# Rotary attention: probabilities turned by VectorE in 32x32 blocks, values multiplied in 32-row tiles, one head per group

## The reference, cut to what matters

```python
xn = layernorm(layernorm(x)) * ln_gamma + ln_beta
q, k, v = split(xn @ w_qkv)                      # 16 heads of 64 each
q, k = rope(q[1:]), rope(k[1:])                  # position 0 stays as it is
dots = einsum('bhqd,bhkd->bhqk', q, k) * 64 ** -0.5
attn = softmax(dots, axis=-1)
out = einsum('bhqk,bhkd->bhqd', attn, v)
x = x + out.reshape(B, N, 16 * 64) @ w_out       # then the other three layers
```

## Time and profile before

| What | Value |
|---|---|
| median of 3 runs | 1472.25 us (1471.01 to 1474.55) |
| the profiled execution's own time | 1474.61 us |
| its span | 1471.4 us |
| mean granted TensorE clock over the span | 0.923 |
| first to last row maximum of the rotary layer | 35.9 to 894.2 us |
| last addition of the rotary layer | 903.64 to 904.06 us |

### The profile page before, as it was taken

The page is one execution under the profiler, slowest core; times in us unless marked ns, Lnnn a source line. Parts: engine busy times, 40 slices in busy tenths (PEclk is TensorE's granted clock), DMA queues, the critical chain, the costliest instruction groups (busy, mean ns, idle before and its releaser), DMA issues. The chain is left out here.

```text
span 1471.4 us, 25634 instructions
## 1 busy us (share of the span) xinstructions
PE 1295.3 (88%) x8965; PEld 918.6 (62%) x8966; DVE 785.1 (53%) x1375; ACT 884.4 (60%) x1567; POOL 269.0 (18%) x200
## 2 busy tenths in 40 slices
PE   4999999999999999999999996279179999999885
PEld 2777777777777776777777774246156455554443
DVE  6555554545554653554554554235357667666616
ACT  4777776777777776777776774323022556555643
POOL 2313312322312321320330330300400000000000
PEclk8999999999999999999999998589675999999987
DMA  6435334334434523523533532611134411011001
GB/s 182 103 92 124 80 81 114 92 75 111 112 75 99 120 61 93 122 61 92 122 80 73 122 86 63 213 41 48 46 93 141 148 48 51 19 42 30 16 1 34
DMA packets 60223, 125.43 MB, mean 85 GB/s; under 512 B 10961, under 2 KB 31826, under 8 KB 59986
## 3 DMA queue, kind: packets, MB, share of 16 engines
q1 hardware_dynamic: 58690, 120.12, 31.7%
q0 software_dynamic: 1424, 3.67, 0.9%
HBM read 31.15 MB, written 13.70 MB: 30 GB/s over the span
## 5 line engine op out<-in xcount | busy, mean ns | idle before, releaser
L529 DVE TENSOR_REDUCE a_negmax<-a_score 128x1 f32<-128x1024 f32 x257 | 314.0, 1222 | 397.0 <-PE a_score L355 397.0
L464 ACT ACTIVATE a_probs_T<-a_tr 128x512 f32<-128x512 f32 x514 | 279.9, 601 | 214.7 <-PE a_tr L361 211.2
L470 ACT ACTIVATE a_probs<-a_score,a_negmax 128x1024 f32<-128x1024 f32 x256 | 288.3, 1126 | 6.8 <-DVE a_negmax L529 6.7
L361 PE MATMUL a_tr<-ident,a_probs 128*128 128x128 f32 x2056 | 269.6, 274 | 0.4 <-ACT a_probs_T L464 0.4
L361 PEld LDWEIGHTS a_tr<-ident,a_probs 128*128 128x128 f32 x2056 | 239.6, 141 | 41.0 <-issue 10.6
L369 PE MATMUL a_out<-a_probs_T,a_v 128*64 128x256 f32 x2112 | 242.5, 382 | 0.5 <-issue 0.5
L1418 ACT ACTIVATE a_probs_T<-a_score_T 128x1024 f32<-128x1024 f32 (+1 forms) x192 | 146.5, 810 | 134.8 <-PE a_score_T L1312 97.2
L1448 DVE TENSOR_REDUCE a_lowest<-a_score 128x1 f32<-128x512 f32 (+3 forms) x320 | 181.6, 629 | 79.3 <-PE a_score L1336 39.2
L369 PEld LDWEIGHTS a_out<-a_probs_T,a_v 128*64 128x64 f32 x2112 | 146.0, 137 | 78.0 <-issue 10.7
L316 POOL TENSOR_TENSOR a_rden<-a_rden_col,a_ones 128x256 f32<-128x256 f32 x65 | 68.3, 1051 | 595.9 <-DVE a_rden_col L552 595.9
L1332 PE MATMUL a_score<-a_k_cur,a_q_still 61*128 61x512 f32 (+3 forms) x320 | 103.6, 435 | 8.6 <-DVE a_lowest L1448 6.9
(11 more groups left out here) (254 smaller groups left out, 1870.6 us busy)
## 6 DMA issues: line engine op xcount, KB each, us to landing
a_xn_cur<-normed_T SPq DMA_DIRECT2D x17, 512.0 KB, 5.1
a_q_rot<-a_q_raw SPq DMA_DIRECT2D x68, 128.0 KB, 2.5
a_k_rot<-a_k_raw SPq DMA_DIRECT2D x68, 128.0 KB, 2.3
a_k_stack1ah<-a_k_hi SPq DMA_DIRECT2D x16, 256.0 KB, 3.3
a_k_stack1al<-a_k_lo SPq DMA_DIRECT2D x16, 256.0 KB, 4.7
a_k_stack1bh<-a_k_hi SPq DMA_DIRECT2D x16, 256.0 KB, 5.0
a_k_stack1bl<-a_k_lo SPq DMA_DIRECT2D x16, 256.0 KB, 4.7
a_k_stack0ah<-a_k_hi SPq DMA_DIRECT2D x16, 256.0 KB, 3.3
```

The lines of the kernel that those rows point to most:

```text
L361: last = nc.tensor.transpose(tr_ps[k // 4][:, k % 4 * P:k % 4 * P + P], probs[s % 4][:, k * P:k * P + P], core.ident[:])
L464: nc.scalar.activation(probs_T[(s - 1) // 4 % 2][:, h, 4 * i:4 * i + 4, tile % 2 * P:tile % 2 * P + P], tr_ps[i][:].rearrange("p (k q) -> ...
L470: nc.scalar.activation(probs[s % 4][:], score_ps[s % 2][:], ACT.Exp, bias=negmax[:, s:s + 1], accum_out=den[:, s:s + 1]).then_inc(probs_re ...
L529: nc.vector.tensor_reduce(negmax[:, s:s + 1], score_ps[s % 2][:], axis=AX.X, op=ALU.max, negate=True)\
```

## The change

The slots of a pair are put in another order: all 8 tiles of head a, then all 8 of head b (`h, tile = s // TB, s % TB`). A group is now one head.

- `transposes`, `copy_tr`, `tr_ps` and all that spread and turned the denominators are gone.
- VectorE turns each tile of probabilities as 4x32 blocks of 32x32, from `probs` into `probs_T[h]` (`turn_blocks`), with one instruction. The blocks stay in their 32 partitions: partitions 32a to 32a+31 hold, for the queries 32a to 32a+31 of every tile, all 32 blocks of keys.
- `values` multiplies 32 keys at a time: 128 products of 32 partitions by 64 columns by 256 queries for a head, spread over four slots, 32 in each. Row tile a (four of them) writes bank a of `acc_ps`, and the keys' two halves c write the partitions 0 to 63 and 64 to 127. The values lie in `v_rep[h]` four times, once in each 32 partitions; they get there through the DRAM tensor `v_rows` (`store_v`, `load_v`).
- ScalarE copies the result of a head in two pieces (`keep_attention`). `project_out` multiplies it with `wo_cur[h]`, which holds the 64 rows of the head twice and so adds the two halves of the keys; there are 16 products for a pair, 8 before. VectorE adds each 128x128 product, times the inverted denominator, to the residual (`add_projected`).
- The rotation of the next pair (four products, two sums) and the low parts are made by GpSimd alone. The stacks exist once; the next pair's queries and keys of a head are written in the half of the pair that works on the other head. The high parts are made by ScalarE (`high_part`).

```diff
+                def turn_blocks(s):
+                    h, tile = s // TB, s % TB
+                    nc.vector.transpose(out=probs_T[h][:, :, 32 * tile:32 * tile + 32], in_=probs[s % 2][:].rearrange("p (b k) -> p b k", b=KB))\
+                        .then_inc(probs_turned, 1)
-                def transposes(s):
-                    for k in range(TB):
-                        last = nc.tensor.transpose(tr_ps[k // 4][:, k % 4 * P:k % 4 * P + P],
-                                                   probs[s % 4][:, k * P:k * P + P], core.ident[:])
-                        if k % 4 == 3:
-                            last.then_inc(tr_ready[k // 4], 1)
-
-                def values(held, weights):
-                    for k in range(TB):
-                        for h in range(2):
-                            ins = nc.tensor.matmul(out_ps[64 * h:64 * h + 64, 0:256], held[:, k, 64 * h:64 * h + 64], weights[:, h, k, :],
-                                                   start=k == 0, stop=k == TB - 1)
-                    ins.then_inc(pv_done, 1)
+                def values(h, steps, done):
+                    for i in steps:
+                        for c in range(2):
+                            block_ = i + KB_HALF * c
+                            v_block = block_ % 4 * TB + block_ // 4
+                            for a in range(4):
+                                rows = slice(32 * a, 32 * a + 32)
+                                ins = nc.tensor.matmul(acc_ps[64 * c:64 * c + 64, a, 0:TB * 32], v_rep[h][rows, v_block, :], probs_T[h][rows, block_, :],
+                                                       start=i == 0, stop=i == KB_HALF - 1)
+                    if done:
+                        ins.then_inc(pv_done, 1)
...
+                    if r in PV_SLOTS and not (first and h == 0) and not (tail and h == 1):
+                        if r == PV_SLOTS[0]:
+                            pe.wait_ge(probs_turned, count(p, SLOTS, TB * h))
+                            pe.wait_ge(v_loaded[1 - h], count(p, V_PARTS, V_PARTS * h))
+                            pe.wait_ge(added, count(p, 4, 2 * h))
+                            pe.wait_ge(item_kept, ITEMS * (PAIRS + 1) if tail else count(p, ITEMS, (ITEMS + 4, 2 * ITEMS)[h]))
+                        chunk = KB_HALF // len(PV_SLOTS)
+                        k = PV_SLOTS.index(r)
+                        values(1 - h, range(k * chunk, k * chunk + chunk), r == PV_SLOTS[-1])
...
+                def add_projected(h, j, batch):
+                    for t in range(4):
+                        tile = 4 * j + t
...
+                        ins = nc.vector.scalar_tensor_tensor(out=row, in0=acc_ps[:, j, t * P:t * P + P], scalar=rden[h][:, tile:tile + 1], in1=row,
+                                                             op0=ALU.mult, op1=ALU.add)
+                    ins.then_inc(added, 1)
...
+                def rotate(i, p):
+                    pool.wait_ge(lo_ready[1][0], count(p, 1, 0))
+                    pool.wait_ge(swapped[i], count(p, 64, 64))
+                    nc.gpsimd.tensor_tensor(raw[i][:], raw[i][:], tables[:, 0, :], ALU.mult).then_inc(rotated[i], 1)
+                    nc.gpsimd.tensor_tensor(rot[i][:], rot[i][:], tables[:, 1, :], ALU.mult).then_inc(rotated[i], 1)
+                    pool.wait_ge(rotated[i], count(p, 2, 2))
+                    pool.wait_ge(hi_ready[1][i], count(p, 1, 0))
+                    nc.gpsimd.tensor_tensor(turned[i][:], raw[i][:], rot[i][:], ALU.add).then_inc(summed[i], 1)
```

More of the change, by code:

```diff
@@ new lines, in rotary_attention, with count, run @@
+        PV_SLOTS = (2, 3, 4, 5)
+        LOOP_FROM = 10
+        def count(p, per_pair, c):
+            it, k = p
+            return k * per_pair + c if it is None else it * per_pair + (k * per_pair + c)
+        def run(engine, slot):
+            for s in range(LOOP_FROM):
+                slot((None, 0), s, first=True)
+            with engine.Fori(0, PAIRS - 1) as it:
+                for s in range(LOOP_FROM, SLOTS):
+                    slot((it, 0), s)
+                for s in range(LOOP_FROM):
+                    slot((it, 1), s)
+            for s in range(LOOP_FROM, SLOTS):
+                slot((None, PAIRS - 1), s, last=True)
+            for s in range(LOOP_FROM):
+                slot((None, PAIRS), s, tail=True)
@@ L220, in rotary_attention, with item_at @@
+        def first_bank(k):
+            return score_ps[k // 2][:, k % 2 * 512:k % 2 * 512 + 512] if k < 4 else acc_ps[:, k - 2, :]
+        def item_at(p, s, first, last, tail):
+            if tail or (last and s >= LOOP_FROM):
+                return None
+            ahead, j = (FIRST_ITEM_SLOTS if first else ITEM_SLOTS).get(s, (None, None))
+            return None if j is None else (j, count(p, ITEMS, ITEMS * ahead + j))
         with nc.Block() as block:
@@ L291, in _ @@
+                sp.wait_ge(w_loaded, 16 * (PAIRS + 2))
+                sp.wait_ge(xn_loaded, 16 * (PAIRS + 1))
+                sp.wait_ge(v_stored, V_PARTS * (PAIRS + 1))
+                for i in range(2):
+                    sp.wait_ge(swapped[i], 64 * (PAIRS + 1))
             @block.gpsimd
@@ L336, in _ @@
+                with pool.Fori(0, PAIRS - 1) as it:
+                    p = (it, 1)
+                    for i in range(2):
+                        rotate(i, p)
+                    for h in range(2):
+                        for i in (1, 0):
+                            rest(h, i, p)
                 pool.wait_ge(slots_cleared, 16)
@@ L437, in _ @@
                 turn_normed(1)
[L438 removed]
+                for k in range(4, ITEMS):
                     project_v(k - 4, first_bank(k), core.xT)
[L440 to L447 removed]
@@ L448, in _ @@
-                pe.wait_ge(zeroed, 2)
-                with pe.Fori(0, PAIRS2) as it:
-                    for par in range(2):
-                        for s in range(SLOTS):
-                            slot(s, par, progress(it, par), ITEM)
-                for s in range(8):
-                    slot(s, 0, LAST, LAST_ITEM, last=True)
+                pe.wait_ge(item_kept, 4)
+                pe.wait_ge(stacked[0], STACKED)
+                scores(0)
+                run(pe, slot)
             @block.scalar
@@ L1641, in rope_tables @@
     cos, sin = np.tile(np.cos(ang), (4, 1)), np.tile(np.concatenate([-np.sin(ang), np.sin(ang)]), (2, 1))
[L1642 to L1643 removed]
+    return np.stack([cos, sin]).astype(np.float32)
 def block_consts():
```

552 lines of the change are left out of this document (263 added, 289 removed).

## The result

The changed kernel takes **1381.31 us**, the median of 4 runs (1378.72 to 1383.71), against 1471.63 (1468.55 to 1474.55, 4 runs) for the kernel before: a ratio of 0.9386, 95% interval 0.9359 to 0.9414. It is faster by 90 us; the prediction said 1378. The profiled execution took 1383.71 us, its span is 1382.0.

The account below looks back on a forecast made before the run. TensorE, 98% busy, was taken to bound the rotary loop. Loop 855.5 to 739 us and end 0.6 more gave 1358.7; hand-overs (7) and clock (14) led to 1380, stated as 1378; range 1345 to 1600, forecast's own 1350 to 1405.

Parts of the forecast that it names:

- Values, eight tiles side by side, 64 rows in 1.73 + 0.35 us: TensorE's slots with values: eight rows share 0.216 us, 0.35 for going in and out; with scores, 3.00 us a slot.
- The rival with tiles in rounds: TensorE's values: the eight tiles go in two rounds, 221 us more, 1600 us; chance 0.14 for tiles not sharing one place.
- the price per product of 46 ns: Rival in TensorE's values: rows issue no faster than 0.046 us each, 159 us more, 1537 us; chance 0.07.
- The turn, 1.22 us: VectorE's turn of one 128x1024 float32 tile, SBUF to SBUF: 1.22 us, with 0.68 and twice 1.22 as ends.
- The bound of 2.44: Rival in VectorE's turn: it costs 2.44 us, making every slot VectorE's, 1640 us; chance 0.06.
- the lock rival: VectorE and GpSimd shut each other out of SBUF during turns: some 130 us more, 1510 us; chance 0.09.
- VectorE's slots: Slots where VectorE sets the pace: maximum and turn 2.44 us, 3.49 with four additions, 3.66 with the inverse too.
- The first values wait for additions or ScalarE: Start of a head's values on TensorE: 2.3 us in after additions, or 3.25 us in after ScalarE's exponential and copy.
- The head, 23.2 us, with 0.2 for hand-overs and 0.45 for the clock: One head of the loop: mean 23.2 us where eight slots took 26.7, with hand-overs and clock on top.
- The clock, 14 us: TensorE's granted clock in the loop: 14 us lost; as a rival, half clock in thin slots, 1430 us, chance 0.12.
- The end, 13.3 us: From the layer's last exponential to its last addition: 13.3 us where it took 12.7, 0.6 more.
- Stacks and SyncE's queue at nothing: Stack transfers and SyncE's queue in the loop: covered by about one slot of 3 us, so costed at nothing.

Follow-up runs that it names:

- run 1: Changed kernel with the products with the values issued one 32-row tile after another: 2276.5 us, ratio 1.548.
- run 2: Changed kernel with all value products of one column half before the other, four tiles side by side instead of eight: 1488.3 us, ratio 1.009.
- run 4: Changed kernel with all value products issued, each streaming 128 columns of the turned probabilities instead of 256: 1327.3 us, ratio 0.902.
- run 5: Changed kernel with VectorE turning half of each tile's blocks, the turned half multiplied twice: 1352.0 us, ratio 0.919.
- run 12: The kernel of run 10 with the values put back from six slots to four, its order of additions, items and copy kept: 1343.4 us, ratio 0.913.
- run 7: Changed kernel with one score product of the tiles of slots 9 and 10 done three times, filling TensorE's idle time: 1377.5 us, ratio 0.934.
- run 6: Changed kernel with one of four score products done twice in every slot without values: 1381.5 us, ratio 0.936.
- run 10: Changed kernel with values spread over six slots, and output projections, additions, items and the accumulators' copy reordered: 1312.9 us, ratio 0.892.
- run 11: The kernel of run 10 with ScalarE making head a's high parts in slots 9 and 10, not 10 and 11: 1312.7 us, ratio 0.893.

## Why the prediction was right

It said 1378 and the kernel takes 1381.3. By its steps:

- **Values, eight tiles side by side, 64 rows in 1.73 + 0.35 us.** Right: eight rows start 6.7 ns apart (not the 4 that the prediction quotes), the next eight 0.216 us later (405.112 to 405.159, then 405.328), 1.98 us in all and a slot of 3.04 against 3.00. Runs 1, 2 and 4 show that it is the tiles side by side, and the columns, that set it. The rival with tiles in rounds is out, and so is the price per product of 46 ns: the rows come at 25. The Trainium skill, "TensorE: Matmul & The Clock Gate", section "Wait — 56ns, not 53.3ns?", has 62 ns for a MATMUL decoded in software; here 64 rows in a row started 25 ns apart in the mean, so that figure is no bound in this kernel; how its products are decoded no run shows.
- **The turn, 1.22 us.** Right: 1.226. The bound of 2.44 is out, and 0.70, near that of 0.68, is what half a turn takes (run 5). No turn grew beside GpSimd (256 turns of 1.18 to 1.25 us), whose operations keep their 2.38 us, so the lock rival is out.
- **VectorE's slots.** 2.44 us was too long: two operations that follow each other overlap, and the distance is 2.26. VectorE's eight distances of a pair, summed at 24.1 us (four of 2.44, two of 3.49 and two of 3.66), took 23.1, although 0 and 8, at 2.61 and 2.50 us, did not reach 2.26.
- **The first values wait for additions or ScalarE.** Right in kind, and it is the weak point of the kernel: TensorE waits 33.2 and 28.1 us for them in all. Run 12, without these waits, is 38 us shorter, but more than half of that is the clock, which fell behind the first of them; pairs of run 7 with the same wait and no fall pay nothing for it in distance 11.
- **The head, 23.2 us, with 0.2 for hand-overs and 0.45 for the clock.** 23.9 measured (47.82 / 2), the same as the sum, but by two errors that cancel: 47.82 us less a fall's 1.4 to 1.6 is 46.2 to 46.4 for a pair, where the terms without the clock gave 46.8, and the clock took 0.7 to 0.8 us of a head and not 0.45. (The hand-overs, 8 of 0.04 us in 31 heads, are 10 us and not the 7 of the sum.)
- **The clock, 14 us.** Too small, and the form was another: 20 to 24 us by the pairs of runs 5 to 7 with and without a fall. I expected a mean between 0.93 and 0.99 over TensorE's part; it is one fall to half in every pair, behind the 2 us that TensorE rests. The loop as a whole came out at 758.6 us against 760, so the slots were summed some 7 to 11 us too long and the clock 6 to 10 too short. That these cancel, and the total with them, is luck; the mechanisms of the slots are not.
- **The end, 13.3 us.** Wrong in size: 17.1. The sum began the last head's values right after the turn; they wait 3.53 us for eight additions of the head before, and take 8.85 us and not 7.3, with the clock at 0.81. Against the sum of 1380 the end has 3.8 us more, the layers behind it, which the change doesn't touch, 2.9, and the loop 1.4 less (758.6 against 760).
- **Stacks and SyncE's queue at nothing.** Right: from 60 us on TensorE waited once for a stack, 0.7 us. The cover is about as thin as said: with slots shorter by 9% (run 10) the transfer came 1.0 us late in each pair, though other work hid it (run 11). How much GpSimd's work could grow was not tried.

Behind this result stands one that I had not seen. Neither engine's total sets the loop (TensorE 90%, VectorE 87%): each sets its own slots, and 38 us more hung on the order of the work at the turn of a head, in good part through the clock.

## What to carry to other kernels

When two engines are each busy for some 90% of a loop, halving the work of one gives less than the sum says: here 58 and 54 us of 109, and 29 of 81. Write down the distances slot by slot, find those that belong to neither, and look at what an in-order engine waits for with another's input queued behind it. Put the work that others wait for first, gather what must wait in one place, and only then spread the long work thinner: spreading over five slots cost 44 us here, and spreading over six after the reordering gained 31. Small products should be issued so that all tiles of the array are in turn before one comes again; the same products in another order cost 107 or 895 us. And when the clock falls in some rounds of a loop and not in others, compare the rounds: that prices it without another run.

## What the runs showed of the hardware that was not expected

- Products for free tiles start beside products still queued for a busy one: with one column half after the other 64 rows took 2.52 us instead of 16 x 0.216 = 3.46.
- The granted clock can fall while TensorE is busy without a gap: 8.30 busy of 8.30 us at 0.50, with about three of eight tiles at work at once (run 1); it stayed at 1.0 with five or six (run 2). In run 1 it was at 1.0 for some stretches of the same work, so what decides is not shown.
- In the changed kernel a rest of 2 us just ahead of 64 rows of values, after slots with TensorE busy for 1.83 of 4.50 us, was followed by half the clock in these rows, in all 15 pairs; with two more products ahead of each of two slots (run 7) the same rest of 1.97 us was followed by it in 11 of 15. With the rest gone (run 10) the clock did not fall once from 75 to 726 us, at TensorE busy for 98%, nor in run 12, at 91% (618.62 of 679 us).
